# Window attention of a fused six-layer transformer: scores on row halves in two banks, probabilities turned in even sub-steps, the FFN in one bank with its first block and the norm's spreading a sub-step later

## The reference, cut to what matters

```python
def attn_layer(x, Wqkv, qs, ksc, Wo):            # 16 heads of 64
    q, k, v = split(x @ Wqkv)
    q, k = rotary(l2norm(q) * qs), rotary(l2norm(k) * ksc)
    out = local_attention(q, k, v)
    return out @ Wo
def local_attention(q, k, v):                    # windows of 32 tokens
    ...                                          # bk2, bv2: the window before and its own, 64 keys
    sim = einsum('bhwie,bhwje->bhwij', bq, bk2) * 8.0
    sim = where(mask, -max, sim)
    attn = softmax(sim, -1)
    return einsum('bhwij,bhwje->bhwie', attn, bv2)
def ffn_layer(x, g, bln, W1, b1, W2, b2):        # inner width 341
    xn = layernorm(x) * g + bln
    a, gate = split(xn @ W1 + b1)
    return a * gelu(gate) @ W2 + b2
for i in range(6):
    x = attn_layer(shift_tokens(x), ...) + x
    x = ffn_layer(shift_tokens(x), ...) + x
```

## Time and profile before

| | us |
|---|---|
| median of 3 runs | 2550.38 |
| lowest, highest | 2549.81, 2551.78 |
| the profiled execution | 2551.92 |
| its span, first to last instruction | 2550.0 |
| TensorE busy in the span | 2372.7 (93%) |
| DVE, POOL, ACT busy | 1768.2 (69%), 1604.3 (63%), 1502.6 (59%) |

### The profile page before, as it was taken

The page is one execution under the profiler, slowest core; times in us unless marked ns, Lnnn a source line. Parts: engine busy times, 40 slices in busy tenths (PEclk is TensorE's granted clock), DMA queues, the critical chain, the costliest instruction groups (busy, mean ns, idle before and its releaser), DMA issues.

```text
span 2550.0 us, 69539 instructions
## 1 busy us (share of the span) xinstructions
PE 2372.7 (93%) x28798; PEld 1592.7 (62%) x28799; DVE 1768.2 (69%) x2707; ACT 1502.6 (59%) x2970; POOL 1604.3 (63%) x931
## 2 busy tenths in 40 slices
PE   5669999999999999999999999999997888889998
PEld 3435666666666666666666666666665666656665
DVE  2348778777877778777877787777865888843232
ACT  1126667666666667666766666666763666643333
POOL 0039888888888888888888888888862222201111
PEclk8879999999999999999999999999997999989999
DMA  4001111111121111211121111211113000000000
GB/s 109 0 9 36 29 33 48 49 38 32 35 55 49 30 34 37 58 38 33 32 56 46 33 33 41 56 40 33 29 28 100 1 1 1 1 1 5 5 3 6
DMA packets 77240, 83.13 MB, mean 33 GB/s; under 512 B 24948, under 2 KB 48770, under 8 KB 76930
## 3 DMA queue, kind: packets, MB, share of 16 engines
q1 hardware_dynamic: 76930, 78.70, 12.1%
HBM read 26.56 MB, written 1.07 MB: 11 GB/s over the span
## 4 chain that ended last, share of the span: by engine, by line
PE 44%; DVE 27%; issue 14%; ACT 11%; POOL 3%; DMA 0%; SPq 0%; ACTq 0%; POOLq 0%; DVEq 0%
DVE qk L1214 7%; PE bank L608 7%; PE bank L819 4%; PE bank L563 4%; PE bank L622 4%; ACT qk L906 4%; PE bank L527 3%; DVE n L1221 3%; PE bank L630 3%; DVE sh L1230 3%; DVE mx L1226 3%; PE obank L829 2%; PE bank L829 2%; PE obank L597 2%; DVE ao L1252 2%
## 5 line engine op out<-in xcount | busy, mean ns | idle before, releaser
L1214 DVE TENSOR_TENSOR qk<-bank,tab 128x1024 f32<-128x1024 f32 x384 | 469.3, 1222 | 246.0 <-ACT qk L906 245.6
L1525 POOL TENSOR_TENSOR qk<-qk 128x1024 f32<-128x1024 f32 x192 | 454.3, 2366 | 227.9 <-DVE qk L1214 227.9
L1529 POOL TENSOR_TENSOR rn<-n2m,cst 128x16 f32<-128x16 f32 x192 | 562.9, 2932 | 16.0
L527 PE MATMUL bank<-wqk,xs 128*128 128x512 f32 x768 | 404.5, 609 | 6.3 <-DMA xs<-Z 3.7
L906 ACT ACTIVATE qk<-bank 128x512 f32<-128x512 f32 x384 | 226.6, 590 | 272.5 <-PE bank L527 272.5
L1533 POOL TENSOR_TENSOR qk<-qk,rn 128x1024 f32<-128x1024 f32 x192 | 365.5, 1904 | 28.1 <-POOL rn L1529 0.9
L538 PEld LDWEIGHTS bank<-cst,qk 128*128 128x128 f32 x1536 | 192.1, 141 | 211.3 <-issue 186.5
L1537 POOL TENSOR_TENSOR lnr<-lnv,cst 128x2 f32<-128x2 f32 (+1 forms) x88 | 66.4, 755 | 388.1 <-DVE lnv L1109 388.1
L538 PE MATMUL bank<-cst,qk 128*128 128x128 f32 x1536 | 231.7, 274 | 8.1 <-POOL qk L1533 8.1
L1221 DVE TENSOR_REDUCE n<-qk 128x16 f32<-128x1024 f32 x192 | 232.2, 1209 | 0.0
L548 PE MATMUL lnbank<-wv,xs 128*64 128x512 f32 x768 | 208.0, 620 | 0.0
(11 more groups left out here) (193 smaller groups left out, 4430.6 us busy)
## 6 DMA issues: line engine op xcount, KB each, us to landing
vp<-vp SPq DMA_DIRECT2D x672, 65.0 KB, 2.0
wqk<-in_L_ffn_Wqkv SPq DMA_DIRECT2D x24, 256.0 KB, 3.4
wv<-in_L_ffn_Wqkv SPq DMA_DIRECT2D x6, 512.0 KB, 3.8
wo<-in_L_ffn_Wo SPq DMA_DIRECT2D x6, 512.0 KB, 4.0
xs<-Z SPq DMA_DIRECT2D x48, 64.0 KB, 2.0
xs<-Z SPq DMA_DIRECT2D x48, 63.8 KB, 2.0
kT<-rel_by_distance SPq DMA_DIRECT2D x1, 2048.0 KB, 8.0
vp<-in_L_ffn_w SPq DMA_DIRECT2D x1, 2048.0 KB, 13.4
```

Source lines behind the costliest of these rows:

```text
L527: nc.tensor.matmul(bank[s % 2][:, :], xs[:, odd, WIN + r * P:WIN + r * P + P], wqk[:, lo:lo + 512], start=True, stop=True).then_inc(p_full, 1)
L1214: tt(qk[:, both, :].rearrange("p o (h d) -> p o h d", d=DH), heads(bank[c % 2][:, :]).unsqueeze(1).broadcast_to([P, 2, PAIRS, DH]), table. ...
L1525: tt(direct, direct, swapped, ALU.add).then_inc(sum_done, 1)
L1529: tt(rn[:, m % 2, :], n2m[:, :], const("mhalf"), ALU.pow).then_inc(rn_done, 1)
```

## The change

1. **Scores.** `kT` loses its zeros: one copy of 128 rows instead of two of 64. A pair's two heads are two matmuls, each over its own 64 rows with 64 key columns, and go to the two banks of a new tile `sbank` (the former banks 3 and 4). DVE's maximum, subtraction and mask take both banks in one operation each.
2. **Turned probabilities.** They go to the first bank of `obank` and from the odd sub-steps to the even ones, behind the turned outputs; so does ACT's copy. `weigh` stands ahead of `values`. ACT's exponential of group 0 in sub-step 7 stands behind squares and key copy instead of ahead.
3. **FFN.** All blocks are in bank 2. The norm's spreading goes from sub-step 3 to 4, hidden(0) from the end of 4 into 5; hidden(1) waits for gate(0) and hidden(2) for gate(1). DVE's scaling of the norm stands behind `parts` in sub-step 4.
4. **Second attention.** `kT` is now too small for the position bias; half of it goes there and half into `tab`, by two DMAs. SP waits ahead of them for the last `parts` as well.

The core of the diff:

```diff
-HD_BANK = (2, 4, 2)
...
-        bank = [ctx.enter_context(nc.psum_tensor(f"bank{i}", [P, 512], F32)) for i in range(5)]
+        bank = [ctx.enter_context(nc.psum_tensor(f"bank{i}", [P, 512], F32)) for i in range(3)]
+        sbank = ctx.enter_context(nc.psum_tensor("sbank", [P, 2, 512], F32))
+        bank += [sbank[:, 0, :], sbank[:, 1, :]]
...
-        kT = sb("kT", [P, PAIRS, 2, KW])
+        kT = sb("kT", [P, PAIRS, KW])
...
+            sp.wait_ge(parts_done, 8 * ITEMS)
+            for half in range(2):
+                sp.dma_start(bias[half], bass.AP(relu_dram.ap().tensor, half * PAIRS * 384, [[1, P], [384, PAIRS], [1, S]]))\
+                    .then_inc(rel_in, 16)
...
                 for q in range(4):
                     for w in range(4):
                         lo = r * P + w * WIN
-                        keys = kT[:, 4 * g + q, :, lo:lo + 2 * WIN].rearrange("p o (s j) -> p o s j", s=2)
-                        mm = nc.tensor.matmul(s[WIN * w:WIN * w + WIN, q * P:q * P + P], qT[:, 4 * g + q, lo:lo + WIN],
-                                              keys if w % 2 else keys[:, :, ::-1, :], start=False, stop=True,
-                                              skip_group_check=True)
+                        for o in range(2):
+                            own = slice(64 * o, 64 * o + 64)
+                            keys = kT[own, 4 * g + q, lo:lo + 2 * WIN].rearrange("p (s j) -> p s j", s=2)
+                            mm = nc.tensor.matmul(sbank[WIN * w:WIN * w + WIN, o, q * DH:q * DH + DH],
+                                                  qT[own, 4 * g + q, lo:lo + WIN],
+                                                  keys if w % 2 else keys[:, ::-1, :], start=False, stop=True,
+                                                  skip_group_check=True)
...
             def turn_probs(i, k):
                 pe.wait_ge(px_done, 4 * i + k + 1)
-                wait(pe, pt_done, 4 * i + k)
-                if k == 0 and i >= 2:
-                    pe.wait_ge(h_done, 3 * i - 4)
+                wait(pe, ao_done, 4 * i + k)
                 for q in range(4):
-                    mm = nc.tensor.transpose(bank[4][:, q * P:q * P + P], px[:, k % 2, q * P:q * P + P], ident)
+                    mm = nc.tensor.transpose(obank[:, 0, q * P:q * P + P], px[:, k % 2, q * P:q * P + P], ident)
...
-                if c == 1:
-                    pe.wait_ge(pt_done, min(4 * i + 8, 4 * ITEMS))
-                if c == 2:
-                    pe.wait_ge(h_done, 3 * i + 1)
+                else:
+                    pe.wait_ge(h_done, 3 * i + c)
...
-                    if s == 6 and p2:
-                        hidden(f, 1)
+                    if s == 4 and p2:
+                        ln_wide_pe(S, LN_S2 + f, bank[2])
+                    if s in (5, 6) and p2:
+                        hidden(f, s - 5)
...
+                    if s % 2 == 0 and p1:
+                        turn_probs(i, s // 2)
+                    if s % 2 == 1 and p1:
+                        weigh(i, s // 2)
...
-                    nc.scalar.copy(kT[0:64, pairs, 0, lo:lo + P], src[0:64])
-                    last = nc.scalar.copy(kT[64:P, pairs, 1, lo:lo + P], src[64:P])
+                    last = nc.scalar.copy(kT[:, pairs, lo:lo + P], src)
...
-                tt(heads(sh[:, k % 2, :]), heads(bank[b][:, :]), mx[:, k % 2, :].unsqueeze(2).broadcast_to([P, PAIRS, DH]),
-                   ALU.subtract).then_inc(sh_done, 1)
+                tt(by_pair(sh[:, k % 2, :]), sc, m.unsqueeze(3).broadcast_to([P, 2, 4, DH]), ALU.subtract).then_inc(sh_done, 1)
```

More of the change, by code:

```diff
@@ L175, in build @@
         bout = sb("bout", [P, 1])
-        bias = kTf[:, 0:H * S].rearrange("p (h t) -> p h t", h=H)
+        tabf = tab[:, :, :, :, :].rearrange("p l k r d -> p (l k r d)")
+        bias = [f[:, 0:PAIRS * S].rearrange("p (h t) -> p h t", h=PAIRS) for f in (kTf, tabf)]
         relv = sb("relv", [WIN, H])
@@ L557, in scores @@
                 pe.wait_ge(seeded, 4 * i + k + 1)
-                s = bank[3]
                 for q in range(4):
@@ L615, in hidden @@
                     pe.wait_ge(ld_w1, (i // B) * 16 + 16)
-                if c == 1:
-                    pe.wait_ge(pt_done, min(4 * i + 8, 4 * ITEMS))
-                if c == 2:
-                    pe.wait_ge(h_done, 3 * i + 1)
+                else:
+                    pe.wait_ge(h_done, 3 * i + c)
                 n = P if c < 2 else FFR
                 for half in range(2):
-                    mm = nc.tensor.matmul(bank[HD_BANK[c]][0:n, half * S:half * S + S], w1[:, half * FF + c * P:half * FF + c * P + n],
+                    mm = nc.tensor.matmul(bank[2][0:n, half * S:half * S + S], w1[:, half * FF + c * P:half * FF + c * P + n],
                                           lnt[:, S:2 * S], start=True, stop=True)
@@ L668, in step @@
                         ln_var_pe(S, LN_S2 + f, bank[2])
[L669 to L672, removed]
+                    if s == 6 and p2:
+                        hidden(f, 2)
                     if s == 7 and p2:
@@ L676, in _ @@
             pe.wait_ge(masks_cast, 1)
-            nc.tensor.matmul(bank[3][:, :], ident_bf, maskv[:, 0, :], start=True, stop=True).then_inc(seeded, 1)
+            nc.tensor.matmul(bank[3][:, :], ident_bf, maskv[:, 0, :], start=True, stop=True)
+            nc.tensor.matmul(bank[4][:, :], ident_bf, maskv[:, 0, :], start=True, stop=True).then_inc(seeded, 1)
             step(0, 0, True, False, False, False)
@@ L939, in take_probs @@
                 wait(act, o_full, 4 * i + k - 1)
-                nc.scalar.copy(pT[:, k % 2, :], bank[4][:, :]).then_inc(pt_done, 1)
+                nc.scalar.copy(pT[:, k % 2, :], obank[:, 0, :]).then_inc(pt_done, 1)
             def take_out(i, k):
@@ L952, in gelu @@
                 act.wait_ge(hd_full, 3 * i + c + 1)
-                nc.scalar.activation(ge[0:n, c, :], bank[HD_BANK[c]][0:n, S:2 * S], ACT.Gelu,
+                nc.scalar.activation(ge[0:n, c, :], bank[2][0:n, S:2 * S], ACT.Gelu,
                                      bias=b1g[0:n, c, bass.ds(i // B, 1)]).then_inc(ge_done, 1)
@@ L960, in step @@
                         gelu(f, 2)
[L961 to L964, removed]
                     if s == 2 and p2:
@@ L972, in step @@
                         take_turned(i, s + 8 - LAG, s)
+                    if s == 7 and p0:
+                        exps(t, 0)
                     if s in (5, 6) and p2:
@@ L986, in step @@
                         take_out(f, 3)
+                    if s % 2 == 0 and p1:
+                        take_probs(i, s // 2)
                     if s in (0, 2, 4) and p1:
@@ L1237, in seed @@
                     dve.wait_ge(sh_done, n)
-                    nc.vector.tensor_copy(bank[3][:, :], maskv[:, (n % 4) // 2, :]).then_inc(seeded, 1)
-            def by_pair(ap):
-                return ap.rearrange("p (q o n) -> p o q n", o=2, n=DH)
+                    nc.vector.tensor_copy(sbank[:, :, 0:4 * DH], maskv[:, (n % 4) // 2, :].rearrange("p (o n) -> p o n", o=2))\
+                        .then_inc(seeded, 1)
             def divide_out(i, k):
@@ L1269, in gate @@
                 dve.wait_ge(ge_done, 3 * i + c + 1)
-                nc.vector.scalar_tensor_tensor(out=hT[0:n, c, :], in0=bank[HD_BANK[c]][0:n, 0:S], scalar=b1a[0:n, c, l],
+                nc.vector.scalar_tensor_tensor(out=hT[0:n, c, :], in0=bank[2][0:n, 0:S], scalar=b1a[0:n, c, l],
                                                in1=ge[0:n, c, :], op0=ALU.add, op1=ALU.mult).then_inc(h_done, 1)
@@ L1295, in step @@
                         parts(t, s)
+                    if s == 4 and p2:
+                        scale_norm(f)
                     if s == 6 and p2:
@@ L1367, in attend @@
                 part = sh[:, m % 2, :].rearrange("p (h n) -> p h n", n=w)
-                tt(part, bank[3 + m % 2][:, :].rearrange("p (h n) -> p h n", n=w), bias[:, hs[0]:hs[-1] + 1, S - w:S]
-                   if r == 0 else bias[:, hs[0]:hs[-1] + 1, :], ALU.add).then_inc(s3["add"], 1)
+                lo = hs[0] % PAIRS
+                tt(part, bank[3 + m % 2][:, :].rearrange("p (h n) -> p h n", n=w), bias[hs[0] // PAIRS][:, lo:lo + len(hs), S - w:S],
+                   ALU.add).then_inc(s3["add"], 1)
                 dve.wait_ge(s3["add"], NJ * b + m + 1)
```

22 lines of the change are left out of this document (8 added, 14 removed).

## The result

The changed kernel takes 2512.95 us (median of 4 runs, 2510.99 to 2515.83) against 2551.08 us before (median of 4, 2549.81 to 2553.1): a ratio of 0.9851, with a 95% interval of 0.9834 to 0.9868, or 38 us less. Forecast were 2510 us and a range of 2476 to 2547.

What follows compares the result with a forecast made beforehand. TensorE and a DVE/ACT chain of nearly equal length beside it bound the period; 0.95 us less in 46 periods (43.7 us) and 3 us more in the last item turn 2551.9 into 2511, median 2510 us, range 2476 to 2547.

Steps and rivals of the forecast that it cites:

- The form's price: TensorE's scores groups: 32 matmuls of 64 rows and 64 columns take 0.79 us for 1.01, 0.22 less for each of four.
- the weighing row: Trace of TensorE's weighing before the change: 32 matmuls into two banks, 64 records in 0.79 us, taken as the scores' price.
- Turned probabilities: TensorE's turning of probabilities, moved to even sub-steps between full-array groups: 0.43 us for 0.59, 0.16 less for each of four.
- Weighing to values: TensorE's switch from weighing directly to values, which no row shows: taken at nothing, bounds -0.1 to +0.16 us.
- The chain: DVE/ACT links from sub-step 1's projection to gate(0), done at t = 20.33, so hidden(1) gains only 0.51 us.
- GpSimd's rotation: Unchanged GpSimd work ahead of the turning before hidden(1): ends at t = 19.03, so the turning starts near 19.1.
- The wait ahead of hidden(1): TensorE idle before the FFN's second block, released by DVE's gate: some 0.7 us a period.
- The stretch from hidden(1) to the next projection: Second part of the period on TensorE: 15.22 us before, 14.78 after, with hidden(2)'s wait covered.
- TensorE alone as the bound: Rival: each microsecond of TensorE's budget counts, 1.8 us a period less, 2471 us; chance 0.12.
- Scores paced by records: Rival: scores groups slow with their doubled records, 1.64 us each, period 37.7 us, total 2627 us; chance 0.08.
- the halves save nothing: Rival: scores stay at 1.01 us and weighing to values costs 0.16 more, period 35.7, total 2537 us; chance 0.14.
- the tail: Last item's FFN, alone on the engines: its blocks wait for gelu and gate, 2 to 4 us more, 3 taken.

Runs made afterwards that it cites:

- x1_two_copies: Changed kernel, but ACT copies the turned keys in two operations of 64 rows again; 2544.34 us, 0.9968 of the kernel before.
- x11_weigh_spaced: Changed kernel with the weighing of group 2 in sub-step 5 done twice, values between the two; 2512.42 us, 0.9855 of the kernel before.
- x6_hidden2_in_7: Changed kernel with hidden(1) behind sub-step 6's scores and hidden(2), its gelu and gate moved into sub-step 7; 2474.96 us, 0.9691 of the kernel before.
- x2_full_rows: Changed kernel with the scores part undone: zero-padded keys, two copies, 16 matmuls of 128 rows and columns a group; 2566.88 us, 1.0057 of the kernel before.

## Why the prediction was right, point by point

- **The form's price.** Scores at 0.79 from the weighing row: measured 0.79. The 25 ns per matmul of the Trainium skill (TensorE: Matmul & The Clock Gate, Part 1) would have made it 1.6; by the trace, the 64 records of a scores group are 12.3 ns apart on average, so that rule does not hold for this group, which is spread over small tiles.
- **Turned probabilities** at 0.43: measured 0.44. **Weighing to values** at nothing: 0.79 stays 0.79.
- **The chain.** gate(0) releases hidden(1) at t = 20.32 for 20.33 forecast, and x1_two_copies shows the chain by lengthening only ACT's part of it. The turning ahead of it starts at t = 1022.62 - 1003.52 = 19.10, as forecast, but in part by luck. I had TensorE there at 18.85 and GpSimd's rotation holding it to 19.1. GpSimd was done at 18.92 and held nothing. TensorE itself came later than my sum, mainly because the turned outputs of sub-step 4 wait some 0.18 us for DVE's division of the group before (the scores group ahead of them takes 0.98 there from start to start), which I had missed; it lies in the slack and costs nothing. The wait ahead of hidden(1) is shown as 0.61 us; from start to start the turning stands 1.22 ahead of it, and 0.44 in x11_weigh_spaced, so it costs 0.78, for 0.7 forecast.
- **The stretch from hidden(1) to the next projection:** 35.11 - 20.32 = 14.79 for 14.78. No wait ahead of hidden(2). TensorE's share in the middle is 98.0%, as forecast.
- **TensorE alone as the bound** (2471) is refuted twice, by x1_two_copies and by x11_weigh_spaced, for this order; x6_hidden2_in_7, where the waits are gone, comes to 2475. **Scores paced by records** and **the halves save nothing** are refuted by the row of 0.79 and by x2_full_rows.
- **Mis-sized: the tail.** I put 3 us, in a range of 2 to 4, to the last item's FFN. It was 4.0 up to the contraction (9.4 for 5.4 us) and 1.3 in the contraction, 5.3 in all. The step that failed is that I priced the waits and left the clock as it was in the row before, where it rose to the upper level 3 us after the first block started, and the contraction had it. With the waits between, all blocks and the contraction ran at the lower level. The part behind item 47's projection grew by 9.5 us in all, the other 4 being spread of the last stages. Against it stood 44.5 us from the periods for 43.7, and 1.5 us before item 0, of which I had expected nothing and which is spread as well. That the total is 2513 for 2510 owes something to these.
- **Over-general:** the second key copy was put at 0.58 us, in sub-step 5 alone. It cost 0.71 us: another 0.13 appear ahead of the exponential, probably from sub-step 1, where the longer copies hold up the norm's mean.
- **Also off: the doubled weighing.** It was put at 0.79 us in sub-step 7 and took 0.65 there, 1.44 for 0.79.

## What to carry to other kernels

An engine that is busy 99% need not be the bound: here a chain over two engines that were busy 79 and 68% of the time ran beside it, and of some 1.75 us a period that TensorE's groups and waits gave up only 0.96 came through. Lay the other engines' rows out from one event of the period to the next, and look for links that begin where the last one ended; what is cut there counts, what is cut from TensorE ahead of the meeting point does not. Where a wait is left, put work of the next group in it before making anything faster: the 38 us of x6_hidden2_in_7 needed no operation less. And a step that is cheap in the steady state should be priced again where it stands alone, with the clock that it gets there.

## What the hardware showed that I had not expected

- In or right behind a burst of 128 small matmul records with their weight loads in sub-step 5, TensorE stood still for 0.2 to 1.3 us in some every fourth period, with the idle put down to issue; with the burst in sub-step 7 it did so in three of 45. Bursts of 64 records, as scores and weighing are, show nothing of the kind, and 128 in one sub-step with values between don't either (longest period 35.41 us).
- Two weighing groups back to back in sub-step 7 took 1.44 us, not twice 0.79.
- Four matmul records of a block took 1.03 us in the steady state, at a granted clock of 1.00, and 2.00 to 2.08 in the last item alone, where TensorE had idled 1.08 to 1.68 us ahead of each and the clock was 0.50.
